# A graph network on one core: 13 node slots per tile, PE's branch ahead of its last three steps, the normalisation's last product on GpSimd

## What is computed

```python
edge_index = jnp.stack([src, dst])
h = jnp.maximum(_layernorm(x, axis=-1), 0.0)
x = x + _L0_gnn_ref(h, edge_index, edge_weight1, edge_attr_3, edge_attr_5, L0_gnn_W)
h = jnp.maximum(_layernorm(x, axis=-1), 0.0)
x = x + _L1_gnn_ref(h, weight, w_comp, self_loop_weight, A1_w, A1_b, A2_w, A2_b, rel_emb, src, dst, edge_type_86)
```

## Time and profile before

| what | value |
|---|---|
| median of 3 runs | 4620.91 us |
| profiled execution, time | 4637.38 us |
| profiled execution, span from first to last instruction | 4635.5 us |
| start, to PE's first find | 0 to 63 us |
| first layer's edge loop | 63 to 2129 us |
| between the layers | 2129 to 2219 us |
| second layer's edge loop | 2219 to 4615 us |
| output | 4615 to 4635.5 us |
| busy: PE, DVE, ACT, POOL | 77%, 58%, 24%, 50% |
| mean granted clock of PE, share of full | 0.851 |

### The profile page before, as it was taken

The page is one execution under the profiler, slowest core; times in us unless marked ns, Lnnn a source line. Parts: engine busy times, 40 slices in busy tenths (PEclk is TensorE's granted clock), DMA queues, the critical chain, the costliest instruction groups (busy, mean ns, idle before and its releaser), DMA issues.

```text
span 4635.5 us, 106735 instructions
## 1 busy us (share of the span) xinstructions
PE 3578.4 (77%) x41254; PEld 3052.1 (66%) x41254; DVE 2689.9 (58%) x3863; ACT 1097.0 (24%) x2563; POOL 2301.7 (50%) x2427
## 2 busy tenths in 40 slices
PE   3788888888888888885677777777777777777777
PEld 2677777777777777775566666666666666666666
DVE  5455555555555555555555665656656665556565
ACT  1111111111111111112233333333333333333332
POOL 5555555555555555553344444544444444445442
PEclk9889988888988989997788888888888888888887
DMA  3111111111111111111122222222222222222221
GB/s 102 21 21 20 20 21 19 20 20 21 20 20 21 20 20 21 21 20 54 35 38 39 38 37 38 40 37 37 37 41 37 38 39 38 37 37 39 39 37 35
DMA packets 216608, 150.09 MB, mean 32 GB/s; under 512 B 121048, under 2 KB 197261, under 8 KB 216079
## 3 DMA queue, kind: packets, MB, share of 16 engines
q0 software_dynamic: 77504, 39.84, 8.9%
q1 hardware_dynamic: 137999, 100.77, 8.8%
q10 hardware_dynamic: 576, 2.40, 0.1%
HBM read 134.58 MB, written 8.22 MB: 31 GB/s over the span
## 4 chain that ended last, share of the span: by engine, by line
PE 38%; issue 13%; another core or an unknown queue 2%; DVE 1%; ACT 1%; ACTq 0%; DVEq 0%
PE ps L636 20%; PE ps L717 7%; PE ps L649 5%; PE ps L675 2%; PE ps L699 1%; PE ps L687 1%; PE ps L599 0%; ACT p_left L846 0%; PE ps L619 0%; DVE room L1095 0%; DVE row_var L969 0%; ACT p_left L886 0%; DVE squares L996 0%; DVE H L966 0%
## 5 line engine op out<-in xcount | busy, mean ns | idle before, releaser
L564 POOL DMA_INDIRECT xg<-h_table,idx x2422 | 2290.8, 946 | 2272.7 <-PE ps L717 1530.1
L636 PE MATMUL ps<-h,blocks 128*128 128x448 f32 x9856 | 2284.3, 388 | 43.3 <-DVE blocks L1024 29.2
L636 PEld LDWEIGHTS ps<-h,blocks 128*128 128x128 f32 x9856 | 1937.9, 202 | 262.8 <-issue 76.6
L1024 DVE TENSOR_TENSOR blocks<-scratch,ps 128x896 fp32r<-128x896 int16 x704 | 761.2, 1082 | 882.8 <-remote 864.7
L717 PE MATMUL ps<-room,xg 128*32 128x42 f32 (+2 forms) x21882 | 699.4, 267 | 301.5 <-issue 297.4
L717 PEld LDWEIGHTS ps<-room,xg 128*32 128x32 f32 x21882 | 579.6, 144 | 429.0 <-issue 412.4
L1033 DVE SCALAR_TENSOR_TENSOR scratch<-ramp_sb,scratch,ps 128x448 f32<-128x448 f32 x704 | 476.4, 677 | 512.1 <-remote 250.7
L649 PE MATMUL ps<-att_tab,p_left 128*128 128x49 bf16 x4689 | 261.2, 200 | 555.3 <-issue 553.7
L1095 DVE TENSOR_TENSOR room<-coef,ps 128x756 f32<-128x756 f32 (+1 forms) x522 | 648.9, 1284 | 4.9 <-DVE ps L1044 0.2
L649 PEld LDWEIGHTS ps<-att_tab,p_left 128*128 128x128 bf16 x4689 | 201.6, 107 | 610.5 <-issue 609.5
L880 ACT ACTIVATE p_left<-ps 96x504 f32<-96x504 f32 (+2 forms) x262 | 168.8, 644 | 1200.8 <-PE ps L717 1200.7
(11 more groups left out here) (108 smaller groups left out, 1144.5 us busy)
## 6 DMA issues: line engine op xcount, KB each, us to landing
xg<-h_table,idx POOLq DMA_INDIRECT x2422
rows_b<-typ_short SPq DMA_DIRECT2D x130, 258.0 KB
scratch<-q_short SPq DMA_DIRECT2D x260, 96.0 KB
rows_b<-dst_short SPq DMA_DIRECT2D x130, 126.0 KB
coef<-in_edge_dram SPq DMA_DIRECT2D x130, 54.0 KB
att_tab<-p_table SPq DMA_DIRECT2D x393, 8.1 KB
p_table<-room SPq DMA_DIRECT2D x8, 297.0 KB
X<-in_x_dram SPq DMA_DIRECT2D x7, 224.0 KB, 4.3
```

What stands on the lines that cost most here:

```text
L564: pool.indirect_dma_start(xg[:, g.q, t - g.s * J, :], None, h_table[n], bass.IndirectOffsetOnAxis(ap=idx[:, t:t + 1], axis=0)).then_inc(L. ...
L636: last = pe.matmul(found_ps[b], blocks[:, b, c, :], h_2[:, a, c], start=(c == 0 and a == 0), stop=(c == NCH - 1 and a == 1))
L1024: dve.tensor_tensor(blocks[:, b], q_b[:, g.b, i, :].unsqueeze(1).broadcast_to([P, NCH, P]), block_ps.unsqueeze(2).broadcast_to([P, NCH, P] ...
```

## The change

WN goes from 14 to 13, and with it every tile's slots in `nodes`, `spread`, the sums and their copies. PE's steps are unrolled in two parts: those up to NG - 2 before the branch, and the last three (`last`) behind it, and once more inside the branch, ahead of the general passes. DVE's last product of the normalisation is split: ACT forms the relu, behind the square of the same chunk, and POOL multiplies by the reciprocal (`scale_rows`), ahead of its gathers. `split_rows` waits for `h_set`. `aggT` is cleared by ACT, ahead of its `split_rows(0)`, by copying a zero tile of bf16 over it.

```diff
-WN = 14
+WN = 13
-def all_steps(eng, body, lag, look):
-
-    for s in range(NG + lag):
-        if s == LOOP[0] * TWELVE:
-            too_far = look(eng)
+def some_steps(steps, body, lag):
+
+    for s in steps:
         body([Group(0, s - d, 0) if 0 <= s - d < NG else None for d in range(lag + 1)])
-    return too_far
...
-        def all_passes(eng, passes, restart=None, finish=None):
+        def all_passes(eng, passes, restart=None, finish=None, last=None):
 
             too_far = passes(0)
             with eng.If(too_far):
+                if last:
+                    last()
                 if restart:
                     restart()
                 with eng.Fori(1, PASSES + 1) as k:
                     passes(k)
                 if finish:
                     finish()
+            if last:
+
+                last()
...
-            pool.memset(aggT[:], 0.0).then_inc(agg_cleared, 1)
+            def scale_rows(n):
+
+                for c in range(NCH):
+                    at = slice(c * MC, (c + 1) * MC)
+                    pool.wait_ge(rstd_set, n * NCH + c + 1)
+                    pool.wait_ge(relu_set, n * NCH + c + 1)
+                    pool.tensor_tensor(h_rows[n][:, at, :], h_rows[n][:, at, :],
+                                       row_rstd[:, at].unsqueeze(2).broadcast_to([P, MC, F]), ALU.mult).then_inc(h_set, 1)
+
             pool.wait_ge(idx_in, 16)
             for n in range(2):
 
+                scale_rows(n)
                 pool.wait_ge(h_stored[n], 16 * NCH)
                 edge_gathers(n)
...
-                    return all_steps(pe, step, 2, look_beyond)
-
-                all_passes(pe, one_pass, None, lambda: pe.wait_ge(L.added, (PASSES + 1) * NG))
+                    some_steps(range(LOOP[0] * TWELVE), step, 2)
+                    too_far = look_beyond(pe)
+                    some_steps(range(LOOP[0] * TWELVE, NG - 1), step, 2)
+                    return too_far
+
+                all_passes(pe, one_pass, None, lambda: pe.wait_ge(L.added, (PASSES + 1) * NG),
+                           lambda: some_steps(range(NG - 1, NG + 2), step, 2))
...
-                    act.activation(squares[:, c % 2], H[:, c * MC:(c + 1) * MC, :], ACT.Square).then_inc(squares_set, 1)
+                    at = slice(c * MC, (c + 1) * MC)
+                    act.activation(squares[:, c % 2], H[:, at, :], ACT.Square).then_inc(squares_set, 1)
+                    act.wait_ge(squares_set, n * NCH + c + 1)
+                    act.activation(h_rows[n][:, at, :], H[:, at, :], ACT.Relu).then_inc(relu_set, 1)
...
+            act.wait_ge(pad_zero, 1)
+            act.activation(aggT[:].rearrange("p (a k) -> p a k", k=3 * KA),
+                           zero[0:3 * F].unsqueeze(1).broadcast_to([3 * F, P, 3 * KA]), ACT.Copy).then_inc(agg_cleared, 1)
             split_rows(0)
...
-                    if c >= 2:
-
-                        dve.wait_ge(rstd_set, o - 2)
-                        dve.wait_ge(squares_set, o - 2)
-                        dve.scalar_tensor_tensor(out=h_rows[n][:, old, :], in0=H[:, old, :], scalar=0.0,
-                                                 in1=row_rstd[:, old].unsqueeze(2).broadcast_to([P, MC, F]),
-                                                 op0=ALU.max, op1=ALU.mult).then_inc(h_set, 1)
...
+                    dve.wait_ge(h_set, o)
```

More of the change, by code:

```diff
@@ L344, in build @@
         sum_set, centred_set, squares_set, var_set = sem("sum_set"), sem("centred_set"), sem("squares_set"), sem("var_set")
+        relu_set = sem("relu_set")
         std_set, rstd_set, h_set = sem("std_set"), sem("rstd_set"), sem("h_set")
```

## The result

| | before | after |
|---|---|---|
| time, median | 4624.3 us (5 runs, 4615.0 to 4628.9) | 4594.0 us (5 runs, 4589.4 to 4597.3) |
| profiled execution, span | 4635.5 us | 4592.2 us |
| mean granted clock of PE | 0.851 | 0.848 |

The ratio is 0.9939 with a 95% interval of 0.9925 to 0.9953: 30.3 us less, where 30.0 were forecast. The two profiled executions differ by more, 43.3 us, because that of before lies 13 us over its median.

A forecast was written before the change was run, and what follows sets the result against it. Bound: both loops' ring of POOL's gathers, standstill and PE's tail. Start +7.0 - 0.7, first loop -9, between layers -4.6 + 3.5 - 1.3, second loop -19.5, end -5.2 + 1.3, drains -1.5: -30.0, 4590.9 us; range 4566 to 4616.

The forecast's parts named there:

- The ring: Edge-loop step: gathers, 1.9 us standstill, PE's tail, about 1 us to the next gather; only PE's tail can shorten it.
- 13 slots in the second loop: PE's sums there pace 2.1 us of each step; 7.1% fewer columns save 0.15 us, times 131: -19.5 us.
- DVE's spread and the other shrunken rows: Shrink by 7.1%; worth nothing in the first loop, about -1.5 us in the last steps of both layers together.
- Sums cleared by ScalarE: At the start, ACT's clear takes 9.6 us and delays the work behind it; all of it shows, +7.0 us.
- Last product on POOL: In the normalisations, POOL's product takes 1.0 us; gains 0.7 us at the start and 1.3 us between the layers.
- PE's branch: Moved ahead of each layer's last three steps: -4.6 and -5.2 us behind the drains, +3.5 and +1.3 us within them.
- The sum: All terms from start to end together: -30.0 us, set against the median of 4620.9 us, 4590.9 us.
- (a): PE's sums are paced by instructions or weight loads, not columns; loops give nothing, -1.5 us, 4619 us; 9%.
- (b): DVE's spread is in the ring too; 0.15 and 0.24 us more off each step, some 50 us, 4541; 6%.
- (c): PE's low clock stretches shift onto the loops' tails; slower, sum +13 to about +55 us, up to 4676; 6%.
- (d): ACT's clear at the start takes 27 us by another row's rate; sum -12 us, 4609 us; 8%.
- (e): Moving PE's branch doesn't do what it should, the holes stay; sum -21 us, 4600 us; 9%.

The follow-up runs named there:

- after_again: The changed kernel itself, timed again on chip B: 3143.5 us, 0.9969 of the kernel before.
- w12: The changed kernel with 12 slots instead of 13, on chip A: 3131.5 us, 0.9934 of the kernel before.
- candidate: The changed kernel with 12 slots, ACT's clear moved into its earlier idle time and the first layer's branch put back, chip C: 4512.3 us, 0.9907 of before.
- clear_early: The changed kernel with ACT's clear ahead of its wait for the transposed indices, chip B: 3136.2 us, 0.9945 of the kernel before.
- w13_alone: The kernel before with 13 slots and nothing else, on chip A: 3134.8 us, 0.9946 of the kernel before.
- branch_alone: The kernel before with PE's branch moved ahead of the last three steps and nothing else, chip A: 3153.5 us, 1.0004 of before.

## Why the prediction was right, point by point

**The ring.** Right for the condition it was read in. The pause shrank by 0.09 us in the first loop (forecast 0.08), and the slots alone gave -33.0 us on chip D. The prediction took the standstill for a property of the kernel. It is not: on chips A and B the same program has none, the second loop is bound by POOL's pace, and the same slots give -17.3 us, all from the first loop and the drains. The forecast would have missed there: after_again is 9.2 us faster than before, not 30.

**13 slots in the second loop.** Mechanism and size held. "2.1 us, 7.1% is 0.15" was too low in the paced part and too high in the share, and the two cancel: the sums' matmuls take 2.72 us of a pause before and 2.57 after, 0.15 less. The pause is 0.23 us shorter in the trace; the rest is in the placing (0.02), in the attention's last matmuls (0.04) and in the end of the standstill (0.03), which the forecast didn't have. In this loop the standstill ends 2.1 us after the last gather, in both kernels, and not 1.9. The timed difference and chip D (33.0 us for both loops and the drains) say that the ordinary gain of this loop is nearer to 20 than to 31 us; the interval of either is some 7 us to each side.

**DVE's spread and the other shrunken rows.** Worth nothing in the first loop, as said: the spread doubled, it cost 0.7 us on B (no difference), and on D the kernel with it stood where the change stands.

**Sums cleared by ScalarE.** The duration was right to 1.2 us. The step that failed is "Nothing else is in the way, so all of it shows: +7.0 us". What was in the way is in the prediction's own first part: a long burst of gathers, and here POOL issues 40 of them on end until 79.9 us. The clear shows in full where nothing is held (7.2 us), and as 1.5 to 2.6 us of the first sum's start where they are.

**Last product on POOL.** 1134 ns in the first normalisation and 940 ns in the second, forecast 1.0 us. The gain to the first gather is 1.1 us, forecast 1.3. The Trainium skill, "GPSIMD Engine Reference", prices it at 0.98 us by the estimate in the prediction; both rows are within 16% of that.

**PE's branch.** Forecast -5.0 us, on chip A +1.3. Both holes moved as forecast, and the jump cost 3.5 and 4.3 us. Two steps failed. In the first layer's drain, "+3.5" has the jump itself right (+2.7, measured 2.7) and what stands behind it wrong: 4.0 us instead of 0.8, since the granted clock there was half, where it had been full. In the second layer's, "L717 waits for the spread until 4602.08 anyway" took the spread's time as fixed. It waits for ACT's attention, and that for PE behind the jump, so the sum came 3.1 us later and not 1.3. The Trainium skill, "Runtime: NRT & Kernel Launch", section "Instruction fetch mechanics", says a taken branch out of the window must fetch its page; the trace agrees that the stall goes with the branch and is moved, not removed.

**The sum.** -30.3 measured, with an interval of -22 to -35, and -30.0 forecast: that they agree to 0.3 us is luck. Two errors cancel: the start was 5 us too dear, the branch 4 (the result's traces) to 6 us (chip A) too favourable. The terms of the loops were right in themselves.

**The rivals.** (a) fell on chip A and on D. (b) fell on B and D for the first layer, where it asked for 104 us; for the second it was not tried, but the 33.0 us of the slots alone leave no room for its 50 more. (c), the clock: the mean granted clock went from 0.851 to 0.848, and the stretches from 300 to 2000 us and from 2300 to 4500 from 0.90 and 0.82 to 0.88 and 0.83; some shift, no cost that the pauses show. (d) fell: 10.75 us. (e) fell as stated, the holes did move, but its time for this term (no gain) was nearer than the forecast's.

All kernels with 12 slots did better than the changed one, as far as different chips can be compared: w12 by 12 us on unheld chips (3131.5 on A, 3143.5 on B), candidate with 0.9907 of before on a held one, where the changed kernel has 0.9939. clear_early beats it by 7.2 us on one chip, at the same 13 slots.

## What to carry to other kernels

Ask of a delay whether something that runs anyway ends later: at the start, nearly seven of eight microseconds vanished behind a burst of gathers that the prediction had itself found to stop the other engines. A stall moved into a stretch of dense matmuls can cost, besides its own length, the lower clock for what follows, as in the first layer here. And a profile is of one chip in one condition: pauses that make up nearly a third of the time were absent on two of the four chips A to D, so take the same kernel's time on several before an order of waits is called a property of the program.

## What the runs showed of the hardware

**Two conditions of a chip.** The same program took 3152 us on two chips and 4553 to 4624 us on three sets of runs elsewhere. In the held condition, towards the end of each burst of 8 to 10 gathers, PE's instructions come 0.7 or 1.4 us apart, until some 1.8 to 2.3 us after the last gather of the second loop's bursts. In the first loop of the changed kernel (100 to 2090 us) 354 of PE's matmuls start more than 0.6 us after the one before. In that of w13_alone on chip A (100 to 1500 us) it is one, though POOL issues gathers without any pause. A gather takes 0.94 us in both. The cause wasn't found.

**A jump of PE and its clock.** Moved ahead of the drains, PE's jump over the general passes shows as a hole of 3.2 to 4.4 us, first layer and second: 3.48 and 4.29 held, and 3.18 and 4.36 on chip A (branch_alone), 3.57 and 4.22 on chip B (after_again). In the first layer the granted clock behind it was at the lower level (0.50 from 2115 us in the changed kernel) and full in the same drain without the jump (1.00 from 2118 to 2126 us in the kernel before).

**ACT at clearing.** Copying a zero row of bf16 by broadcast over 12672 f32 elements took 10.75 us, 0.85 ns per element, where ACT's bf16 rows of 1536 elements take 0.97 ns with their fixed part and POOL's own clear took 10.65 us.
